# A graph network kernel: relu writes PSUM and the scan reads it there, in the first and third pass over the edges

## The reference

```
edge_index = stack([src, dst])
h = max(layernorm(x), 0);  x = x + L0(h, edge_index, edge_weight, ...)
h = max(layernorm(x), 0);  x = x + L1(h, edge_index, ...)      # 4 rounds of graph convolution
h = max(layernorm(x), 0);  x = x + L2(h, node_vec1, edge_index, edge_weight, ...)
h = max(layernorm(x), 0);  x = x + L3(h, edge_index, edge_attr_32, ...)
```

```
neighbors = concat([x[src], x[dst]]);  all_dst = concat([dst, src])
edge_features = neighbors * (1 + coef * ew)
pooled = relu(edge_features @ pool_w.T + pool_b)
pooled = where(all_src != all_dst, pooled, -inf)
agg = maximum(segment_max(pooled, all_dst), 0)
L0 = relu(concat([x, agg]) @ final_w.T + final_b)
```

## Time and profile before

| | before |
|---|---|
| time, median of 3 | 14502.07 us (14379.72 to 14513.35) |
| span of the profiled execution | 12468.1 us |
| PE, DVE, ACT, POOL busy | 65%, 47%, 46%, 47% |
| L648, POOL gathers, 1,664 | 1990.0 us, mean 1196 ns |
| L678, POOL scatters of records, 1,664 | 1697.4 us, mean 1020 ns |
| L714, POOL scatters to adj, 1,664 | 1729.1 us, mean 1039 ns |
| L1673, DVE scan, data in SBUF, 414 | 530.1 us, mean 1281 ns |
| L1264, ACT relu of the first pass, 208 | 143.0 us, mean 687 ns |
| granted TensorE clock, mean | 0.743 |

### The profile page before, as it was taken

The page is one execution under the profiler, slowest core; times in us unless marked ns, Lnnn a source line. Parts: engine busy times, 40 slices in busy tenths (PEclk is TensorE's granted clock), DMA queues, the critical chain, the costliest instruction groups (busy, mean ns, idle before and its releaser), DMA issues.

```text
span 12468.1 us, 199604 instructions
## 1 busy us (share of the span) xinstructions
PE 8143.0 (65%) x68487; PEld 5647.8 (45%) x68487; DVE 5873.6 (47%) x10300; ACT 5780.0 (46%) x8522; POOL 5840.3 (47%) x5419
## 2 busy tenths in 40 slices
PE   3333333328887877162555102999999999995999
PEld 2222222226666665142444101555665555654555
DVE  5555555536666665353655101434344434434444
ACT  1111111115555554151232102888888888883777
POOL 5777777767777777577777776000000000000000
PEclk6555555556667676575566556999999999996999
DMA  4444444423333333993576102766666666663998
GB/s 137 144 144 144 145 144 145 144 76 89 89 90 90 90 88 80 101 279 82 114 159 155 37 0 68 206 205 189 205 206 186 206 205 187 206 198 65 174 175 163
DMA packets 2836837, 1747.96 MB, mean 140 GB/s; under 512 B 1859990, under 2 KB 2689020, under 8 KB 2835924
## 3 DMA queue, kind: packets, MB, share of 16 engines
q1 hardware_dynamic: 2509508, 1305.01, 42.6%
q10 hardware_dynamic: 153360, 277.67, 6.0%
q0 software_dynamic: 173184, 154.23, 5.5%
HBM read 1065.41 MB, written 502.11 MB: 126 GB/s over the span
## 4 chain that ended last, share of the span: by engine, by line
POOL 40%; PE 33%; issue 17%; DMA 4%; DVE 2%; ACT 2%; SPq 1%; POOLq 0%; DVEq 0%; ACTq 0%
PE PS L1059 31%; POOL G L648 14%; POOL adj L714 14%; POOL records L678 11%; DMA AG<-adj 2%; SPq L509 1%; POOL EA L735 1%; ACT AG L1523 1%; POOL AG L696 1%; DMA G<-node_table,IDX 1%; DMA records<-RT,IDX 0%; PE PS L780 0%; PE PS L940 0%; PE PS L1087 0%; DMA dinv_n<-dinv 0%
## 5 line engine op out<-in xcount | busy, mean ns | idle before, releaser
L1059 PE MATMUL PS<-AG,T 128*64 128x512 bf16 (+1 forms) x22064 | 2556.0, 354 | 807.5 <-ACT AG L1434 791.1
L2006 DVE CAST AG<-AG 128x1792 bf16<-128x1792 uint8 x1176 | 1286.8, 1095 | 2661.1 <-PE PS L1059 1628.0
L1434 ACT CAST AG<-AG 128x1792 bf16<-128x1792 uint8 x1176 | 1970.5, 1683 | 827.0 <-DMA AG<-adj 742.1
L648 POOL DMA_INDIRECT G<-node_table,IDX x1664 | 1990.0, 1196 | 601.2 <-issue 596.6
L714 POOL DMA_INDIRECT adj<-OH,EA x1664 | 1729.1, 1039 | 661.2 <-issue 554.9
L1059 PEld LDWEIGHTS PS<-AG,T 128*64 128x64 bf16 x22064 | 1234.6, 110 | 1671.9 <-ACT AG L1434 795.9
L678 POOL DMA_INDIRECT records<-RT,IDX x1664 | 1697.4, 1020 | 530.3 <-issue 500.7
L1059 PE MATMUL PS<-AG,RT 128*64 128x512 bf16 (+1 forms) x11032 | 1504.8, 353 | 0.0
L743 POOL DMA_INDIRECT AG<-node_table,srow x28 | 31.6, 1127 | 2594.3 <-issue 2594.3
L1434 ACT CAST M<-AG 128x1792 bf16<-128x1792 uint8 x588 | 990.8, 1685 | 301.2 <-PE PS L1059 274.9
L940 PE MATMUL PS<-R 98*128 98x128 f32 x3328 | 1023.6, 402 | 0.0
(11 more groups left out here) (371 smaller groups left out, 13972.9 us busy)
## 6 DMA issues: line engine op xcount, KB each, us to landing
AG<-adj SPq DMA_DIRECT2D x2940, 224.0 KB, 2.8
adj<-Z ACTq DMA_DIRECT2D x105, 1568.0 KB, 6.3
G<-records SPq DMA_DIRECT2D x624, 128.0 KB
M<-same_dst SPq DMA_DIRECT2D x416, 128.0 KB
fill_rows<-Z ACTq DMA_DIRECT2D x104, 512.0 KB, 2.6
runs_l<-R SPq DMA_DIRECT2D x208, 256.0 KB, 3.2
G<-fill_rows SPq DMA_DIRECT2D x208, 256.0 KB
runs<-R ACTq DMA_DIRECT2D x208, 256.0 KB, 4.3
```

The costliest lines, as they stand in the source:

```text
L648: pool.indirect_dma_start(G[:, i, q * D:(q + 1) * D], None, table, bass.IndirectOffsetOnAxis(ap=IDX[:, i, q:q + 1], axis=0)).then_inc(sem( ...
L1059: m = pe.matmul(PS[h * D:(h + 1) * D, base + c:base + c + w], stat(t), rhs[:, h * QW + c:h * QW + c + w], start=start and t == 0, stop=sto ...
L1434: act.copy(RING[i], RAW[i]).then_inc(sem("conv_a"), 1)
L2006: dve.tensor_copy(RING[i], RAW[i]).then_inc(sem("conv_d"), 1)
```

## The change

Four lines. In the first pass relu of chunk i writes bank 6 + i % 2 in place of `L[:, i % 2, :]`, and the scan reads its data there; these banks aren't used in this pass. In the third pass relu writes bank 5 * s (0 or 5), s = i % 2, and the scan reads it there; both are unused in that pass too. Tile shapes, semaphores, their values and the order of all instructions stay.

```
-                act.activation(L[:, i % 2, :], bank(i % 2), ACT.Relu, bias=poolb[:, 0:1]).then_inc(sem("pt_free"), 1)
+                act.activation(bank(6 + i % 2), bank(i % 2), ACT.Relu, bias=poolb[:, 0:1]).then_inc(sem("pt_free"), 1)
...
-                act.activation(L[:, s, :], bank(1 + 5 * s), ACT.Relu, bias=poolb[:, 0:1]).then_inc(sem("l3r"), 1)
+                act.activation(bank(5 * s), bank(1 + 5 * s), ACT.Relu, bias=poolb[:, 0:1]).then_inc(sem("l3r"), 1)
...
-                scan(i, n, L[:, i % 2, :], ALU.mult, ALU.max, first).then_inc(sem("scanned"), 1)
+                scan(i, n, bank(6 + i % 2), ALU.mult, ALU.max, first).then_inc(sem("scanned"), 1)
...
-                scan(i, c + N3, L[:, s, :], ALU.mult, ALU.max, first and i == 0).then_inc(sem("scanned"), 1)
+                scan(i, c + N3, bank(5 * s), ALU.mult, ALU.max, first and i == 0).then_inc(sem("scanned"), 1)
```

## The result

The changed kernel takes **14715 us** (median of 4 runs, 14675 to 14922). The kernel before, on the same chip in turn with it, takes 14508 (4 runs, 14380 to 14623). The ratio is **1.018, interval 1.009 to 1.027**, where 14217 and a gain were forecast. Slower by 1 to 2%, then; no gain in any case.

What follows compares the result with a forecast made beforehand. Up to TensorE's part, a row of GpSimd DMA instructions was taken to bound the kernel. Savings of 91 + 194 = 285 us brought the span from 12468.1 to 12183; with 2034 around it, 14217 us, range 14110 to 14400.

Steps and rivals of the forecast that it cites:

- Mechanism: First and third pass: GpSimd issues beginning inside a scan would no longer be held up, none over 0.98 us.
- Third pass: Third pass: GpSimd's scatter issues fall from 1.269 to 0.97 us, saving 91 us, bounds 0 and 91.
- First pass: First pass: GpSimd's gather issues, freed from the scan, save 1.11 us in each of 175 cycles, 194 us, bounds 0 and 231.
- The direct part: First pass: the scan's own hold on a GpSimd issue goes, 0.48 us in each of 175 cycles, 84 us.
- The indirect part: First pass: the next GpSimd issue starts earlier in the one-hot block and takes 1.27 us, not 1.90, saving 0.63 per cycle.
- relu and scan: First and third pass: relu into PSUM takes 0.69 us, the scan from PSUM 1.27 us; both cost zero.
- what lies around the span is 2034 if the profiled execution was like the median: Whole kernel: 14502.1 - 12468.1 = 2034 us lie outside the profiled span and were added to the new span.
- The sum's span, 12183: Whole kernel: the profiled span 12468.1 us less the 285 us saved, 12183 us.
- all on GpSimd's chain: First and third pass: the whole 285 us saved lies on GpSimd's chain; later stages start earlier and last as long.
- The one that ended slower: First pass: GpSimd issues lock into a bad phase, plus 187 us, less 91 in the third pass: 14598 us, chance 0.04.
- the first (L648 above 1.14): First pass: a mean gather issue staying above 1.14 us would show the forecast wrong, the phase having eaten the gain.
- the second, GpSimd waiting at `runs_done(2)`: End of the third pass: GpSimd waiting there for the pass to finish would show the forecast wrong.

Runs made afterwards that it cites:

- after_fourth: The changed kernel, unchanged, run again beside a kernel before of 12450 us: 12196 us, ratio 0.980.
- hold_once_more: Kernel before with the change in the first pass only, plus a second scan over two SBUF inputs behind each scan there: 12448 us, ratio 1.000.
- iota_once_more: Kernel before with the first pass's one-hots reading their column numbers from PSUM, relu and scan left in SBUF: 12150 us, ratio 0.976.
- its first half alone: Kernel before with only the first pass's relu and scan changed, run twice: 14720 us, ratio 1.006, and 14686 us, ratio 1.015.
- the three comparisons: The changed kernel against the kernel before, three times: 14715 us, ratio 1.018; 14767 us, ratio 1.009; 14775 us, ratio 1.020.
- before_again: The kernel before, unchanged, profiled and timed once more against itself: 14626 us, ratio 0.991, or 0.998 by medians of all executions.

## Why the prediction failed

**Mechanism: right, and shown.** Issues inside scans over the PSUM chunk aren't held up. In after_fourth none of them is lengthened, in either pass. One of each:

```profile
1015.02 1.27 DVE L1673 TENSOR_TENSOR_SCAN S<-M,S,PS 128x512 f32<-128x512 bf16 x1
...
1015.62 0.94 POOL L648 DMA_INDIRECT G<-node_table,IDX  x1 [0.30 <-issue]
1016.21 2.22 DVE L1665 TENSOR_TENSOR OH<-iota_b,AG 128x392 bf16<-128x392 bf16 x4
...
1016.87 1.30 POOL L648 DMA_INDIRECT G<-node_table,IDX  x1 [0.30 <-issue]
...
5300.24 1.28 DVE L1673 TENSOR_TENSOR_SCAN S<-M,S,PS 128x512 f32<-128x512 bf16 x1 [2.38 <-ACT PS L1363]
...
5300.43 0.96 POOL L714 DMA_INDIRECT adj<-OH,EA  x1 [0.30 <-issue]
```

And in hold_once_more two scans stand side by side, first the one from PSUM, then the added one from SBUF (its mask is float32, and it adds in place of multiplying):

```profile
1000.39 1.27 DVE L1673 TENSOR_TENSOR_SCAN S<-M,S,PS 128x512 f32<-128x512 bf16 x1
...
1000.99 0.94 POOL L648 DMA_INDIRECT G<-node_table,IDX  x1 [0.31 <-issue]
1001.58 1.20 DVE L1701 TENSOR_TENSOR_SCAN L<-Hn 128x512 f32<-128x512 f32 x1
...
1002.24 1.29 POOL L648 DMA_INDIRECT G<-node_table,IDX  x1 [0.30 <-issue]
```

The iota runs show the same for a plain comparison; iota_once_more has:

```profile
L648 POOL DMA_INDIRECT G<-node_table,IDX x1664 | 1689.6, 1015 | 601.3 <-issue 588.2 <-DMA IDX<-in_src_q 13.1
```

The Trainium skill ("SBUF — State Buffer", Who interferes with whom) ties the contention to two SBUF inputs; by that rule moving one input of the one-hots should free GpSimd, and the trace agrees: a mean of 1.015 to 1.023 us in place of 1.195. Its inference that `tensor_tensor` doesn't stall descriptor generation doesn't hold here.

**Third pass: right in a quiet execution.** Forecast 91 us. The scatters 0 to 415 take 544 us in after_fourth and 633 before, 89 less.

**First pass: the size of one term.** Forecast 194, measured 2496 - 2335 = 161 (of two quiet executions). The direct part, the scan's own hold, was 95 us by my count of the issues inside scans, and all of it went; 84 was forecast for it. The indirect part, that the freed issue meets the one-hots earlier and waits shorter, was taken as 0.63 us in each of 175 cycles, 110 us, and gave 66. The cycle at 1015 above is the forecast one (0.94, then 1.30). But the next phase over is as common:

```profile
1001.40 1.37 POOL L648 DMA_INDIRECT G<-node_table,IDX  x1 [0.30 <-issue]
1001.87 1.27 DVE L1673 TENSOR_TENSOR_SCAN S<-M,S,PS 128x512 f32<-128x512 bf16 x1
...
1003.07 1.34 POOL L648 DMA_INDIRECT G<-node_table,IDX  x1 [0.30 <-issue]
...
1004.72 1.38 POOL L648 DMA_INDIRECT G<-node_table,IDX  x1 [0.30 <-issue]
```

Three issues are each held by some 0.4 us. Over the pass the waits of 0.9 to 1.0 us fell from 210 to 5, and those of about 0.4 rose from 121 to 440. One cycle had been taken for all.

**relu and scan: right.** L1264 takes 662 ns (0.69 taken), scans 1.27 to 1.28.

**The step that failed: "what lies around the span is 2034 if the profiled execution was like the median".** It wasn't. The sum's span, 12183, is within 13 us of what the changed kernel takes in a quiet set (12196), closer than the gain itself (285 forecast, 254 measured): that is luck, since before was 18 us quicker in that set than in the profile. Then 2034 us were added as if they were a constant that no edit could touch, and with them went the assumption that "all on GpSimd's chain" holds in the timed executions too. Between the quiet and the late execution of before (12468 and 14675, 2207 us) the time lies inside the program, where late signals stand in the trace: 954 in the second pass, 353 from the first scatter to the 417th (the third pass), 842 from there to the first issue of L735, 58 elsewhere. In late executions the two gains go like this:
 - The third pass's 91 us are not there to be had, since its scatters already run nearly undisturbed (558 us before, 556 after) and GpSimd then waits for the pass's end.
 - The first pass saves its issue time (173 us), and brings late signals into the one stage that had been free of them; they cost more (231 us). Before 2499 us, after 2529, 2557 and 2586.

So the traces show why nothing was gained, and a loss of 30 to 87 us in the first pass for the change, up to 130 for its first half alone. The measured loss, by the medians of the three comparisons, is 207, 105 and 150 us (by the ratios 0.9 to 2.0%). What is left over isn't tied to a stage. The one late trace of before, 14675, is one of that kernel's longer times and only 49 us shorter than after's 14724; its quicker ones, down to 14377, were not traced, and late executions of one kernel differ by 1 to 2% among themselves.

**The rivals.** The one that ended slower gave 14598 by a bad phase in GpSimd's issues, with a mean above 9.99 us per eight. The mean fell to 8 x 1.094 = 8.75. The sign was that rival's, the mechanism wasn't. Of the two signs that I said would speak against the forecast, the first (L648 above 1.14) did not come; the second, GpSimd waiting at `runs_done(2)`, did, as the idle 6750 to 7000 above shows.

**What could have been read beforehand.** The table of times had a span of 12468 beside three times that start at 14380. Nothing shown then said that 2034 us can't lie around a span; that it is 1.8 us came out with the runs. But the gap was seven times the gain, and was put down to something constant without a row. The range should have had a case for it: that in the timed executions GpSimd isn't what sets the stages' length.

## What to carry to other kernels

Lay the span of the profile beside the timed runs before making a sum; if they differ by more than their spread, profile again and find out which stages differ, because a sum made from one kind of execution holds only for that kind. Where times vary by over 1%, look at all of them before believing a ratio that rests on the quickest. The edit itself is sound where GpSimd's DMA issues bound a stage: give a VectorE instruction beside them at most one input in SBUF, the wider and more frequent ones first (here the one-hots of the first pass alone, 0.976, before the scans of both passes, 0.980). And a quicker producer can lose: look at what it does to those that run beside it, with one experiment that slows it down again and leaves all else in place.

## What was unexpected in the hardware

- **Late signals.** In some sets the semaphore of a matmul changes long after the matmul has ended, in stretches in which GpSimd issues DMAs: the engines that wait start up to 32 us later in the first pass, up to 14 in the second and, with the delays of several steps added up, up to 42 in the third, there at exactly 11.20 us from one to the next. The second pass goes from 2204 to between 3088 and 3179 us, the third (first scan to last) from 489 to between 852 and 1002, and the program from 12450 to 14600. The traces of late executions also hold fewer semaphore records, 130 to 151 thousand for 220 thousand; of the 71 thousand that before_again lacks beside before, 69 thousand are landings of DMAs, most of them of GpSimd's. Both traces hold all 199604 instructions. The cause is open.
- **They go by the pace of GpSimd.** First pass, late starts of 416: 0 at a mean issue of 1190 to 1202 ns, some 75 to 102 at 1090 to 1099, 157 to 173 at 973 to 977, and 0 again when it is slowed to 1197.
- ScalarE's relu of 128x512 takes 662 ns into PSUM and 687 to 688 into SBUF.
- A GpSimd DMA issue that begins inside a scan is held if the scan reads SBUF twice and isn't if it reads PSUM and SBUF. In hold_once_more 173 begin inside the scans from PSUM, none over 0.95 us, and 174 inside the added ones from SBUF, none under 1.27.
